# The order of masked minimum, reciprocal and scaling on VectorE in a fused local-attention kernel

## The reference

```python
value = conv1x1(gn(x), v_w, v_b)
keyf  = proj(gn(x), ...)             # two 1x1 convolutions, each with batch norm and relu
query = proj(gn(x), ...)
uk = concatenate([unfold3(keyf, d) for d in (1, 2, 4)])    # 27 neighbours of a pixel
uv = concatenate([unfold3(value, d) for d in (1, 2, 4)])
sim = softmax(sum(uk * query[:, :, None], axis=1))
x = x + conv1x1(sum(sim * uv, axis=2), w_w, w_b)
```

## Time and profile before

| | |
|---|---|
| median of 3 runs | 1523.75 us (1523.29 to 1524.77) |
| profiled execution | 1524.56 us, span from first to last instruction 1522.8 us |
| instructions | 35364 |
| busy: TensorE / weight loads | 1461.1 us (96%) / 1192.3 us (78%) |
| busy: VectorE / ScalarE / GpSimd | 1213.1 us (80%) / 1166.8 us (77%) / 815.9 us (54%) |
| mean granted TensorE clock | 0.998 |

### The profile page before, as it was taken

One profiled execution on the slowest core, in us unless ns is written; L12 is line 12 of the kernel. 1 busy time (PEld: TensorE's weight loads), 2 busy tenths in 40 slices (PEclk: granted clock), 3 DMA queues, 4 the chain that ended last, 5 costly groups with the idle time before them and its releaser, 6 DMA issues.

```text
span 1522.8 us, 35364 instructions
## 1 busy us (share of the span) xinstructions
PE 1461.1 (96%) x9159; PEld 1192.3 (78%) x9159; DVE 1213.1 (80%) x4631; ACT 1166.8 (77%) x3044; POOL 815.9 (54%) x2313
## 2 busy tenths in 40 slices
PE   1799999999999999999999999999999999999998
PEld 0588888888888888888888888888888888888886
DVE  6488888887888888888888888878888888888775
ACT  2577787877787877787877787877787877787876
POOL 5645565655565645565645565654565645565620
PEclk9999999999999999999999999999999999999999
DMA  2245543455543455543455543454543455543344
GB/s 91 82 115 153 159 123 110 139 159 152 160 123 110 139 160 153 160 123 109 139 161 152 160 123 104 145 161 152 161 123 109 139 160 152 159 125 108 101 116 140
DMA packets 104708, 205.97 MB, mean 135 GB/s; under 512 B 13632, under 2 KB 83776, under 8 KB 96448
## 3 DMA queue, kind: packets, MB, share of 16 engines
q1 hardware_dynamic: 103632, 203.49, 45.1%
q10 hardware_dynamic: 880, 0.23, 0.1%
HBM read 51.62 MB, written 51.38 MB: 68 GB/s over the span
## 4 chain that ended last, share of the span: by engine, by line
PE 81%; issue 6%; ACT 5%; DVE 5%; POOL 2%; ACTq 0%; DVEq 0%; POOLq 0%
PE ps_s L432 20%; PE ps_o L465 17%; PE ps_p L487 11%; PE ps_v L505 10%; PE ps_t L444 9%; PE ps_p L482 9%; PE ps_o L470 3%; ACT e L597 1%; DVE v L1007 1%; ACT kk L640 1%; ACT qq L629 1%; ACT hid L618 1%; DVE e L986 1%; DVE e L969 1%; PE ps_v L533 1%
## 5 line engine op out<-in xcount | busy, mean ns | idle before, releaser
L597 ACT ACTIVATE e<-e,zmin 128x256 f32<-128x256 f32 x800 | 404.0, 505 | 183.1 <-DVE zmin L969 176.3
L465 PEld LDWEIGHTS ps_o<-eT,v 128*128 128x128 f32 x2688 | 380.3, 191 | 86.2 <-issue 81.5
L465 PE MATMUL ps_o<-eT,v 128*128 128x128 f32 x2688 | 433.8, 276 | 0.5 <-ACT eT L612 0.3
L432 PE MATMUL ps_s<-kk,qq 128*128 128x256 f32 x1408 | 425.2, 384 | 0.1
L969 DVE CUSTOM_DVE_ANT_0 e<-ps_s,mask 128x256 f32<-128x256 f32 x800 | 337.2, 421 | 102.2 <-PE ps_s L432 94.2
L444 PE MATMUL ps_t<-ident,e 128*128 128x128 f32 x1600 | 305.9, 273 | 0.2 <-DVE e L986 0.2
L444 PEld LDWEIGHTS ps_t<-ident,e 128*128 128x128 f32 x1600 | 225.2, 141 | 81.1 <-DVE e L986 0.5
L612 ACT ACTIVATE eT<-ps_t 128x512 f32<-128x512 f32 (+1 forms) x416 | 234.9, 565 | 60.1 <-PE ps_t L444 58.6
L432 PEld LDWEIGHTS ps_s<-kk,qq 128*128 128x128 f32 x1408 | 223.4, 191 | 47.8 <-issue 41.2
L986 DVE SCALAR_TENSOR_TENSOR e<-e,rz,keep 128x256 f32<-128x256 f32 x480 | 258.9, 539 | 0.0
L977 DVE RECIPROCAL rz<-zs 128x1 f32<-128x1 f32 x800 | 126.5, 158 | 139.8 <-ACT e L597 130.3
(11 more groups left out here) (150 smaller groups left out, 1815.3 us busy)
## 6 DMA issues: line engine op xcount, KB each, us to landing
out_dram<-raw SPq DMA_DIRECT2D x32, 1568.0 KB, 5.8
raw<-in_x_dram SPq DMA_DIRECT2D x31, 1568.0 KB, 6.7
v<-v SPq DMA_DIRECT2D x192, 224.0 KB, 2.9
kk<-kk SPq DMA_DIRECT2D x192, 112.0 KB, 2.2
ksp<-kk SPq DMA_DIRECT2D x192, 64.0 KB, 2.1
v<-v_last SPq DMA_DIRECT2D x64, 128.0 KB, 2.9
kk<-kk SPq DMA_DIRECT2D x32, 224.0 KB, 2.9
v<-v_last SPq DMA_DIRECT2D x64, 96.0 KB, 2.7
```

What stands on the lines that cost most here:

```text
L432: nc.tensor.matmul(ps_s[i][:, 0:KEYS].rearrange("p (s h k) -> p h s k", s=2, h=2), qq[:, t, :], window.rearrange("p h (s k) -> p h s k", s=2),
L465: last = nc.tensor.matmul(o[:, UPIX * (u - 1):UPIX * (u + 1)], v[:, s, u, :], eT[:, UPIX * (base + 2 * u - 1):UPIX * (base + 2 * u + 1)], ...
L597: nc.scalar.activation(e[:, i, :], e[:, i, :], ACT.Exp, bias=zmin[:, i:i + 1], scale=-1.0, accum_out=zs[:, i:i + 1]).then_inc(e_done.next( ...
```

## The change

VectorE's slot has the same instructions with the same waits. The masked minimum of tile t is issued first, and the reciprocal and the scaling of tile t-1 follow it. Before, the reciprocal stood ahead of the masked minimum and the scaling behind it.

```diff
                     def slot(n, t):
                         if n.offset == first + 1:
                             tables(t)
+                        if n.exists():
+                            masked(n, t)
                         m, k = lagged(n, t, SCALE)
                         if m.exists():
                             reciprocals(m, k)
-                        if n.exists():
-                            masked(n, t)
-                        if m.exists():
                             scaled(m, k)
                         for m, at in chain_at(n, t):
                             chain(m, at)
```

## The result

The changed kernel takes 1504.1 us (median, 1503.82 to 1504.32) against 1524.18 us for the kernel before: ratio 0.9864, interval 0.9852 to 0.9876, 20.1 us less. The forecast was 1506 us in a range of 1498 to 1522. The profiled execution has a span of 1502.4 us against 1522.8.

A forecast was written before the change was run, and what follows sets the result against it. TensorE, busy 45.27 of 45.68 us an image, was taken as the bound. Gains of 0.55 + 0.20 - 0.20 us over 30 images, plus 1.5 at the end, made 18 us: 1506 us forecast, range 1498 to 1522.

The forecast's parts named there:

- Place one: TensorE's L487 waits for ScalarE's hidden layer; earlier masked minima shorten that gap and its restart, 0.55 us an image gained.
- The nearest step alone: Moving only the masked minimum right before the hidden layer's chain brings the hidden layer at least 0.36 us earlier.
- Place two: TensorE's L528 waits for GpSimd steps behind VectorE's L1054; these come earlier, closing the gap: 0.20 us an image gained.
- follow from those instructions' own form and stay: TensorE's remaining gaps, behind matmuls of 1 and 6 columns and before the rim matmul, were taken as unchangeable.
- the bound of 0.83 us: Most the edit can gain an image: 0.60 us at L487 plus 0.23 us at L528.
- Place three: The reciprocal now stands in VectorE's path to the aggregate and GpSimd's L749, releasing TensorE's L521: 0.20 us an image lost.
- The last image: In the last 20 us, without projections, masked no longer waits for the previous exponential: 1.5 us gained, bounds 0 to 2.9.
- Case 2: Rival, chance 0.15: only the nearest step works, exp(B) stays bound by key and query copies; 5 us gained, 1518 to 1519.
- Case 3: Rival, chance 0.13: nothing measurable, since what one TensorE gap gives the next takes back; 1521 to 1526 us.
- Case 4: Rival, chance 0.10: slower; both GpSimd chains start 0.20 us later, delaying L528 and L521, 0.40 us an image, 1536 us.
- the wait for rz: Reciprocal and scaling back to back on VectorE put 0.20 us into every slot where masked waits for scores.
- VectorE's wait for the exponential would move behind masked: Expected sign: VectorE's wait for ScalarE's exponential, 130.3 us before, moves from before the masked minimum to after it.

The follow-up runs named there:

- t = 4 and 5 run: Kernel before, with masked, reciprocal, scaling order only in slots t = 4 and 5 of VectorE's queue: 1514.15 us, ratio 0.9933.
- t = 0 to 3 run: Kernel before, with masked, reciprocal, scaling order only in slots t = 0 to 3 of VectorE's queue: 1510.97 us, ratio 0.9918.
- two runs with the chain steps second: Changed kernel with aggregate and gate steps moved ahead of reciprocal and scaling: in every slot 1501.45 us, in slot t = 12 alone 1494.74 us.

## Why the prediction was right

- **Place one, the hidden layer** (0.55 us an image, bounds 0.36 to 0.60). Right and slightly low: the gap and nearly all of its restart went, 17.6 us over 27 images, 0.65 by the table (in the median, L487 starts 0.45 us behind its predecessors where it was 1.00, and the scores 0.78 behind L487 where it was 0.86: 0.63). The nearest step alone was priced at 0.36 and gave 0.35 (0.55 to 0.20 in the t = 4 and 5 run). That the slots before act on the gap too is shown by the t = 0 to 3 run, where they alone took off 0.36 us.
- **Place two, L528** (0.20, bounds 0 to 0.23). The gap went whole (0.24 us in the median start distance, 0.69 to 0.45; 0.27 by the table), and 0.11 us more in the mean came from the scores behind L528. The step "follow from those instructions' own form and stay" was wrong for this one gap, and with it the bound of 0.83 us: the gap was half a late start. When L528's weights are loaded while the four L465 run (load at 696.90, matmul at 697.01), the next start follows after 0.14 and not 0.24 us (load at 705.10, matmul at 705.13). The two runs with the chain steps second show the same behind L521; with the old order in slot 12 the load still came just late (710.22, matmul at 710.25) and the 0.26 us stayed.
- **Place three, L521** (-0.20). Right: L521 starts 0.67 us behind the first L465 where it was 0.47, in the median -0.20 an image (-0.24 by the table, which counts the new gap from too small a base), 6 us either way when slot 12 alone keeps or takes the new order.
- **Not foreseen:** 0.08 us an image (0.89 to 0.97 us; 0.11 by the table) ahead of the context matmuls behind the value matmuls. The weight load of the value matmuls now waits for VectorE's copy L1057, which stands behind the reciprocal and the scaling; with that copy ahead of them the gap is absent.
- **The last image** (1.5): 1.6 by the trace.
- **The sum.** 0.65 + 0.27 + 0.11 - 0.24 - 0.11 = 0.68 an image from the gap table's places, 0.65 by its total, 0.64 by the length of an image. Thirty images and the end make 21 us, with 20.1 measured and 18 forecast. The forecast is close by its terms, not only in the sum, but two that it had at nothing, +0.11 behind L528 and -0.08 behind the value matmuls, nearly cancel.
- **Rivals.** Case 2 (exp(B) stays tied) fell with the t = 0 to 3 run. Case 3 fell with the result. Case 4's mechanism, the wait for rz put into a slot that waits for scores, is real and is place three; it did not reach L528, whose gap closed; before that slot the wait had been for the exponential. The rule of the Trainium skill ("VectorE: DVE Perf Modes", The DRAIN you can't avoid) that a semaphore between chained instructions is free put L521's loss at 0.15 us; here reciprocal to scaling took 0.20 us (713.79 to 713.99), and the loss was 0.20. The other rule of the Trainium skill, to work on the engine with the highest occupancy ("Perfetto Trace Analysis", Identifying the Most-Contended Engine), holds in this sense: what was gained were gaps of TensorE (51.6 to 34.5 us), though the edit was on VectorE.
- **Wrong:** that VectorE's wait for the exponential would move behind masked. It vanished (130.3 to 0.9 us). The price still came out right; that neither wait was on TensorE's path then is my reading, which no run isolates.

## What to carry to other kernels

When one engine is busy 99% of its steady state, list its gaps from the distances of its starts, follow each to the queue that feeds it, and judge an edit slot by slot: the same swap won 19 us in six slots and lost 6 us in one. In an in-order queue put first what another engine waits for and can already run; put behind it what waits itself. Undo the edit where it loses: with the old order in one slot of 25 the kernel takes 1498.64 us, and with the chain steps ahead of the reciprocal in that slot instead 1494.74 us.

## What the runs showed of the hardware that I had not expected

A late start of a small matmul costs twice. L528 and L521 (6 columns) are followed by the scores after 0.23 to 0.26 us when their weight load starts only 0.03 us before them, and after 0.14 us when it starts 0.11 us before them, behind the matmuls ahead. The value matmuls show the same on a smaller scale: with their load late by 0.1 us, the matmul behind the eight follows after 0.97 and not 0.89 us.

A one-column reciprocal of a constant has a record of 0.156 us, but 800 of them raised VectorE's busy time by 52 us, 0.065 us each, and the next instruction started 0.08 us behind (698.02 to 698.10). Where the next instruction waits for the reciprocal's result the distance is 0.20 us (713.79 to 713.99).
